# The last dense pass of a graph kernel: centring and scaling on ScalarE, column by column, one pair later

## Chip, cores and metric

One core of one Trainium2 chip runs the whole kernel in one launch. The metric is the device time of that launch in microseconds, the median of several runs. PE is the matrix engine (TensorE), DVE is VectorE, ACT is ScalarE, POOL is GpSimd, SP is SyncE, which here only issues DMAs.

## What is computed

A table `x` of 100,000 nodes with 48 features goes through four rounds of messages over 25,000 edges, each followed by a layer norm. What matters here is the fourth:

```python
gate = silu(edge_attr @ W1.T + b1) @ W2.T + b2 + adapt_logit
msg = gate * h[dst] * (cw * node_mult[dst])[:, None]
agg = segment_sum(msg, src, N) / clip(tot, 1e-8)[:, None]
x = h + agg
y = (x - mean(x)) / sqrt(var(x) + 1e-5) * gamma + beta     # _L3_gnn_ref
out = layernorm(h + y)                                      # the last step of reference()
```

The third round has a dense part too: a node without edges gets `relu(b)` added and is normed. A node that no edge writes to needs no messages, so for most of the table rounds three and four together are a row-wise function of the table after round two.

## The kernel before

Nodes lie 784 to a partition (128 partitions), edges 196 to a partition. **Dense passes** run over all nodes in 28 blocks of 28 rows a partition (a tile half of 128x28x48 = 128x1344 f32), two blocks to a pair: SyncE loads both halves of `din`, VectorE and ScalarE work on them, SyncE stores both halves of `do`. **Sparse rounds** run over the edges in 14 chunks of 14 edges a partition (128x14x48 = 128x672). GpSimd gathers each chunk with 14 indirect DMAs, VectorE forms the messages and sums them with a scan, ScalarE spreads masks and copies the sums back. Rows that edges touch are corrected afterwards by an indirect scatter over the dense result.

The change lies in the last dense pass, `dense_pair` on VectorE (L1563 on) and on ScalarE (L753 on). It does round three's norm, round four's norm with gamma and beta for nodes without edges, and the final norm, for 14 pairs. The pairs are put between the chunks of three sparse rounds, in an order written out by hand that both engines' programs must share:

- `REC_PAIRS = 6`: one pair after every second chunk of the **records round** (`records`, L765 and L1594). Chunks are gathered into two ring buffers (L465); GpSimd fills one again when VectorE has read it (L1596) and ScalarE has stored it (L768).
- `SRC_PAIRS = (2, 3, 4, 5)`: one pair after the 3rd to 6th of the seven blocks of the **h2 round** (L1630 on).
- `LAST_PAIRS = 4`: one pair after every second of the first eight chunks of the **terms round** (`terms_of`, L816 and L1643). Its rows are gathered ahead into four ring buffers (L508), each free again when ScalarE has refilled it (L789, L820).

In one pair VectorE adds the bias (L1566), sums the squares that ScalarE makes (L605, L1570), takes two reciprocals for each half (L1573, L1574) of roots from ScalarE (L757, L759), multiplies (L1577), builds the factor from gamma (L1580), applies it (L1584) and adds beta (L1587). Then `norm` takes the mean (L1343), centres (L1346), sums the second squares (L1352), takes reciprocals (L1355) of ScalarE's roots (L611) and writes the product to `do` (L1363). All full-size VectorE operations are 128x1344, twice a pair.

In SyncE's queue `dense` (L382 on) has the loads of pair n+1 ahead of the stores of pair n, and both ahead of the loads of pair n+2. A load waits for `in_free`, a store for `out_ready`.

After the terms round come `carries` (L1319), a last loop over the 14 chunks (L1690 on, `norm_half`) and the scatter to `out` (L520), which waits until all dense stores have landed.

Of the kernel before, what the change touches and what calls it, by code (L numbers as in the profile page):

```python
# [6 lines left out]
P = 128  # L7
D = 48
# [4 lines left out]
CE = 196  # L13
# [15 lines left out]
SORT_C = 256  # L29
REC_PAIRS, SRC_PAIRS, LAST_PAIRS = 6, (2, 3, 4, 5), 4  # L30
SORT_P = EP // SORT_C
# [58 lines left out]
def bass_gnn(nc, A, OUT):  # L90
    ALU, ACT, X = mybir.AluOpType, mybir.ActivationFunctionType, mybir.AxisListType.X
    ctx = ExitStack()
    with ctx:
# [25 lines left out]
        def blk(table, k, w=D):  # L119
# [107 lines left out]
        back = gflat[:, 0:2 * H * RW].rearrange("p (h c w) -> p h c w", h=2, w=RW)  # L227
        put4 = zs[:, :].bitcast(I32)
        PS = ctx.enter_context(nc.psum_tensor("PS", [P, 8 * 512], F32))
        psT0, psT1, psA, psB, psC, psO0, psG, psS = (PS[:, k * 512:(k + 1) * 512] for k in range(8))  # L230
# [28 lines left out]
            "zt_ready", "zt_st", "z_ld0", "z_ld1", "z_free", "h2_fill0", "h2_fill1", "h2_fill2", "h2_fill3",  # L259
            "h2_free") + ROWS}  # L260
        FROM_DMA = ("look", "g_ld", "g_fill", "g_st", "consts", "edges", "ea48", "xa_ld0", "xa_ld1", "ld0", "ld1",
# [311 lines left out]
        def _(act):  # L573
# [177 lines left out]
            by_src = RECB.rearrange("(p c) w -> p c w", p=P)  # L751

            def dense_pair():  # L753
                squares(pair)
                for h in range(2):
                    act.wait_ge(var_ready.sem, var_ready.up())
                    nc.scalar.activation(std[:, h, :], var[:, h, :], ACT.Sqrt, bias=lneps[:, 0:1], scale=1.0 / D  # L757
                                         ).then_inc(own.sem, own.add())
                    nc.scalar.activation(std2[:, h, :], var[:, h, :], ACT.Sqrt, bias=eps2[:, 0:1],  # L759
                                         scale=(1.0 + EPS) / D).then_inc(own.sem, own.add())  # L760
                    act.wait_ge(own.sem, own.now())
                    act.sem_inc(S["std_ready"], 1)
                norm(pair)

# [10 lines left out]

            record_turn = {own: 4, scanned: 2, spread: 4, returned: 2, fill[0]: H, fill[1]: H, rb_st[0]: 1, rb_st[1]: 1}
            act.wait_ge(S["by_src"], 1)
            for i in range(REC_PAIRS):
                for h in range(2):
                    records(2 * i + h, h)  # L780
                dense_pair()
            for i in range(NBLK - REC_PAIRS):
                for h in range(2):
                    records(2 * (i + REC_PAIRS) + h, h)

# [30 lines left out]
            def terms_of(c, h, last=False):  # L816
# [11 lines left out]
                if not last:  # L828
                    load_back(c + 2, h)

            term_turn = {own: 2, scanned: 2, spread: 4, returned: 2, centered: 2, var_ready: 2, ring_read: 2,
                         rb_ld[0]: 1, rb_ld[1]: 1}
            for i in range(LAST_PAIRS):
                for h in range(2):
                    terms_of(2 * i + h, h)
                dense_pair()
            for i in range(NBLK - 1 - LAST_PAIRS):
                for h in range(2):
                    terms_of(2 * (i + LAST_PAIRS) + h, h)
            for h in range(2):  # L840
                terms_of(CE // H - 2 + h, h, True)

# [174 lines left out]
        def _(dve):  # L1017
# [541 lines left out]
            V.tensor_copy(gammaP, rows[:, 1, :]).then_inc(own.sem, own.add())  # L1559
            one(V.tensor_copy(betaP, rows[:, 2, :]))  # L1560
            dve.sem_inc(S["by_src"], 1)

            def dense_pair():  # L1563
                for h in range(2):
                    dve.wait_ge(ld[h].sem, ld[h].up())
                    V.tensor_tensor(DU[h], wide(h, D), down(rbcP), ALU.add).then_inc(S["centered"], 1)  # L1566
                for h in range(2):
                    dve.wait_ge(squared.sem, squared.up())
                    dve.sem_inc(S["in_free"], 1)
                    V.tensor_reduce(var[:, h, :], sq[:, h, :, :], X, ALU.add).then_inc(S["var_ready"], 1)  # L1570
                for h in range(2):
                    dve.wait_ge(std_ready.sem, std_ready.up())
                    V.reciprocal(srsP[:, h, :], std[:, h, :]).then_inc(own.sem, own.add())  # L1573
                    V.reciprocal(sr2[:, h, :], std2[:, h, :]).then_inc(own.sem, own.add())  # L1574
                dve.wait_ge(own.sem, own.now())
                for h in range(2):
                    V.tensor_tensor(DU[h], DU[h], along(srsP[:, h, :]), ALU.mult).then_inc(own.sem, own.add())  # L1577
                    one(V.tensor_tensor(sr2[:, h, :], sr2[:, h, :], std[:, h, :], ALU.mult))
                for h in range(2):
                    V.tensor_tensor(factorP[:, h, :, :], along(sr2[:, h, :]), down(gammaP), ALU.mult  # L1580
                                    ).then_inc(own.sem, own.add())
                dve.wait_ge(own.sem, own.now())
                for h in range(2):
                    V.scalar_tensor_tensor(DU[h], factorP[:, h, :, :], 1.0, DU[h], ALU.add, ALU.mult).then_inc(own.sem, own.add())  # L1584
                dve.wait_ge(own.sem, own.now())
                for h in range(2):
                    V.tensor_tensor(DU[h], DU[h], down(betaP), ALU.add).then_inc(own.sem, own.add())  # L1587
                dve.wait_ge(own.sem, own.now())
                norm(pair, stores=True)
                for h in range(2):  # L1590
                    st[h].n += 16
                dve.sem_inc(S["out_ready"], 2)

# [6 lines left out]

            pair_turn = {ld[0]: 1, ld[1]: 1, st[0]: 1, st[1]: 1, squared: 4, std_ready: 4}
            PAIR = 4 + 4 + 2 + 2 + 2 + NORM2
            record_turn = {fill[0]: H, fill[1]: H, spread: 4, ring_read: 2}
            for i in range(REC_PAIRS):
                for h in range(2):
                    records(h)
                dense_pair()
            for i in range(NBLK - REC_PAIRS):
                for h in range(2):
                    records(h)  # L1610
            dve.wait_ge(returned.sem, returned.up(2 * NBLK))
# [31 lines left out]
            def terms_of(c, h):  # L1643
# [16 lines left out]

            term_turn = {own: 8, fill[0]: H, fill[1]: H, spread: 4, ring_read: 2, squared: 2, std_ready: 2,
                         rb_ld[0]: 1, rb_ld[1]: 1}
            for i in range(LAST_PAIRS):
                for h in range(2):
                    terms_of(2 * i + h, h)
                dense_pair()
            for i in range(NBLK - LAST_PAIRS):
                if i == NBLK - LAST_PAIRS - 1:
                    counts(nv[:, :])
                for h in range(2):  # L1670
                    terms_of(2 * (i + LAST_PAIRS) + h, h)
            dve.wait_ge(returned.sem, returned.up(2 * NBLK))
# [100 lines left out]
```

## Time and profile before

| | us |
|---|---|
| median of three runs | 2563.16 |
| lowest and highest | 2560.93, 2564.61 |
| the profiled execution, its own time | 2565.39 |
| its span in the trace | 2563.4 |
| DVE busy in the span | 1932.9 (75%) |
| POOL busy | 1781.0 (69%) |
| ACT busy | 618.8 (24%) |
| PE busy | 556.7 (22%) |

The profile is one execution. "Busy" counts the instructions' own time; an engine's idle time before an instruction is given with what ended it. In the timeline, a row is a start, a duration, an engine, a line, what is written from what, how many such instructions are merged ("x2"), and in brackets the idle time before it and what ended it. The records round lies between about 1435 and 1720 us, the h2 round and the products before it between 1720 and 2026, the terms round between 2026 and 2277, the last loop and the scatter after that.

### The profile page before, as it was taken

The page shows a single profiled execution, that of the slowest core. Times are in us where ns is not written, and L with a number is a line of the kernel's source. Part 1 is how long each engine was busy: PE and PEld are TensorE (multiplying, and loading weights), DVE is VectorE, ACT ScalarE, POOL GpSimd, SP SyncE. Part 2 cuts the span into 40 slices and gives each one's busy share as a digit, 9 for nine tenths or more (in the row PEclk, how much of TensorE's full clock was granted, in tenths as well). Part 3 has the DMA queues.
Part 4 walks back from the last instruction along what each step waited for, and adds up shares of the span by engine and source line. Part 5 has one row for each costly group of instructions (what it writes and reads, how often), then busy time and mean ns, then how long its engine had stood idle before and what let it go on. Part 6 is the DMA issues. An engine that isn't in the chain of part 4 may idle for free.

```text
span 2563.4 us, 12772 instructions
## 1 busy us (share of the span) xinstructions
PE 556.7 (22%) x2848; PEld 471.7 (18%) x2848; DVE 1932.9 (75%) x2740; ACT 618.8 (24%) x1106; POOL 1781.0 (69%) x1768
## 2 busy tenths in 40 slices
PE   3800000006787375532310000006200000000000
PEld 1300000006777254432310000006200000000000
DVE  5889999997888675553484099984699999988881
ACT  4910022213443221111110023231112222321110
POOL 4777777775777767737776676767777774637776
PEclk9955555556666576755555555555555555555555
DMA  4169589823445333298009644452232222210000
GB/s 137 21 230 329 156 322 330 299 69 111 158 147 168 104 72 69 51 54 56 17 13 67 87 131 142 124 160 63 50 84 79 82 79 83 65 37 17 17 16 15
DMA packets 158466, 276.19 MB, mean 108 GB/s; under 512 B 88601, under 2 KB 113507, under 8 KB 158259
## 3 DMA queue, kind: packets, MB, share of 16 engines
q1 hardware_dynamic: 96675, 206.39, 28.6%
q0 software_dynamic: 56448, 44.23, 10.3%
q10 hardware_dynamic: 5264, 24.74, 2.7%
q8 instruction: 23, 0.38, 0.1%
q14 instruction: 56, 0.46, 0.1%
HBM read 142.41 MB, written 138.17 MB: 109 GB/s over the span
## 4 chain that ended last, share of the span: by engine, by line
DVE 47%; POOL 20%; issue 9%; PE 8%; DMA 8%; ACT 7%; SPq 1%; ACTq 0%; DVEq 0%; POOLq 0%
POOL out L520 7%; POOL ring L465 7%; POOL x_table L520 6%; DVE PS L1343 5%; PE PS L897 5%; DVE du L1346 5%; DVE var L1352 4%; DVE do L1363 3%; DMA x_table<-sumb,put 3%; PE PS L883 3%; DVE sumb L1271 3%; DMA din<-in_xaux 2%; DMA din<-x_table 2%; ACT GX L661 2%; DVE du L1577 2%
## 5 line engine op out<-in xcount | busy, mean ns | idle before, releaser
L605 ACT ACTIVATE sq<-du 128x1344 f32<-128x1344 f32 x129 | 169.2, 1321 | 541.5 <-DVE du L1346 518.5
L520 POOL DMA_INDIRECT x_table<-sumb,put x196 | 212.5, 1084 | 114.1 <-issue 58.2
L508 POOL DMA_INDIRECT ring<-h_by_src,zs x196 | 204.0, 1041 | 98.8 <-issue 58.5
L478 POOL DMA_INDIRECT XD<-in_xaux,srcI x196 | 201.0, 1025 | 86.3 <-issue 59.1
L520 POOL DMA_INDIRECT out<-sumb,put x196 | 192.6, 982 | 96.5 <-issue 61.8
L465 POOL DMA_INDIRECT ring<-x_with_degree,srcI x196 | 203.7, 1039 | 80.4 <-issue 60.6
L520 POOL DMA_INDIRECT x_with_degree<-sumb,put x196 | 193.8, 989 | 86.7 <-issue 57.3
L465 POOL DMA_INDIRECT ring<-edge_records,dstI x196 | 185.9, 949 | 91.4 <-issue 57.9
L478 POOL DMA_INDIRECT XD<-x_table,srcI x196 | 196.3, 1002 | 59.7 <-issue 59.7
L478 POOL DMA_INDIRECT XD<-xa_table,dstI x196 | 191.1, 975 | 59.7 <-issue 59.4
L866 PE MATMUL PS<-ident,tail 128*49 128x128 f32 x10 | 4.5, 447 | 911.1 <-DVEq L1045 911.1
L1352 DVE TENSOR_REDUCE var<-sq 128x28 f32<-128x1344 f32 x105 | 159.0, 1550 | 36.5 <-ACT sq L605 35.6
L897 PE MATMUL PS<-w1c,hT 98*128 98x96 f32 x784 | 155.5, 365 | 77.4 <-ACT hT L624 74.7
L866 PEld LDWEIGHTS PS<-ident,tail 128*49 128x49 f32 x10 | 1.6, 157 | 913.6 <-DVEq L1045 893.3
L897 PEld LDWEIGHTS PS<-w1c,hT 98*128 98x128 f32 x784 | 147.9, 281 | 82.5 <-ACT hT L624 79.5
L624 ACT ACTIVATE hT<-PS 97x512 f32<-97x512 f32 (+3 forms) x168 | 89.8, 541 | 274.0 <-PE PS L883 273.8
L883 PE MATMUL PS<-ident,din 128*97 128x128 f32 x392 | 94.5, 388 | 256.7 <-DMA din<-x_table 256.7
L883 PEld LDWEIGHTS PS<-ident,din 128*97 128x97 f32 x392 | 75.7, 255 | 259.3 <-DMA din<-x_table 259.3
L1343 DVE TENSOR_REDUCE PS<-du 128x28 f32<-128x1344 f32 x73 | 111.1, 1556 | 3.0
L1346 DVE SCALAR_TENSOR_TENSOR du<-PS,du 128x1344 f32<-128x1344 f32 x73 | 111.0, 1553 | 1.4
L597 ACT ACTIVATE MG<-sumb 128x672 f32<-128x672 f32 x42 | 56.7, 1351 | 192.7 <-DVE sumb L1271 192.7
L983 PE MATMUL PS<-logit,du 120*128 120x120 f32 x392 | 69.9, 352 | 81.0 <-DVEq L1471 81.0
(271 smaller groups left out, 2489.7 us busy)
## 6 DMA issues: line engine op xcount, KB each, us to landing
din<-in_xaux SPq DMA_DIRECT2D x56, 728.0 KB, 5.0
xa_table<-din SPq DMA_DIRECT2D x28, 728.0 KB
x_table<-GX SPq DMA_DIRECT2D x28, 686.0 KB
x_with_degree<-GX SPq DMA_DIRECT2D x28, 686.0 KB
din<-x_table SPq DMA_DIRECT2D x28, 686.0 KB
x_table<-do SPq DMA_DIRECT2D x28, 672.0 KB
din<-x_table SPq DMA_DIRECT2D x28, 672.0 KB
out<-do SPq DMA_DIRECT2D x28, 672.0 KB
```

What stands on the lines that cost most here:

```text
L465: pool.indirect_dma_start(ring[:, h, t, 0:w], None, table, bass.IndirectOffsetOnAxis(ap=of[:, c * H + t:c * H + t + 1], axis=0), **skip).t ...
L478: pool.indirect_dma_start(XD[:, t, 0:w], None, table, bass.IndirectOffsetOnAxis(ap=of[:, t:t + 1], axis=0)).then_inc(rows[c].sem, rows[c]. ...
L508: pool.indirect_dma_start(ring4[:, c % 4, t, :], None, H2, bass.IndirectOffsetOnAxis(ap=of[:, c * H + t:c * H + t + 1], axis=0), bounds_ch ...
L520: pool.indirect_dma_start(table, bass.IndirectOffsetOnAxis(ap=put[:, c * H + t:c * H + t + 1], axis=0), rows_of[:, h, t, :], None, bounds_ ...
L605: nc.scalar.activation(sq[:, h, :, :], u, ACT.Square).then_inc(S["squared"], 1)
L624: nc.scalar.activation(hT[0:tall, g % 2, 0:w], psT[g % 2][0:tall, 0:w], ACT.Copy).then_inc(S["hT_ready"], 1)
L883: last = T.transpose(psT[g % 2][0:tall, j * P:(j + 1) * P], rows_of[:, at:at + tall], ident[:, :])
L897: last = T.matmul(psO[k % 5][:, j * 96:(j + 1) * 96], hT[0:tall + 1, g % 2, j * P:(j + 1) * P], weights[:, :], start=True, stop=True)
L1271: return V.tensor_tensor_scan(sums_row[:, part], by[:, :, :].rearrange("p d c -> p (d c)"), terms_row[:, part], 0.0, ALU.mult, ALU.add)
L1343: V.tensor_reduce(mean[:, h, :], x, X, ALU.add).then_inc(own.sem, own.add())
L1346: V.scalar_tensor_tensor(u, along(mean[:, h, :]), -1.0 / D, x, ALU.mult, ALU.add).then_inc(S["centered"], 1)
L1352: V.tensor_reduce(var[:, h, :], sq[:, h, :, :], X, ALU.add).then_inc(S["var_ready"], 1)
```

## The change

In the dense pairs, the second norm's centring and its product leave VectorE. VectorE still takes the mean (now of the row sums `mu`), and the sum of squares, now of the uncentred values; from both it works out the variance, asks ScalarE for one root of 128x56, and leaves a scale `srs` and a shift `mu` for each row. ScalarE applies both in a new function, `final`, by one activation for each of the 28 columns of each half, with the shift as bias and the scale as scale, and writes `do`. It does so for pair n-1 during pair n, between the roots and the second squares, from two buffers `zbuf` in `gflat`. VectorE's second mean in pair n waits for it (`final`), because it overwrites `mu`. The last pair's `final` stands on ScalarE after chunk 12 of the terms round.

Beta is centred once, ahead of the records round. The stores' `out_ready` comes from ScalarE, half by half. The pairs of the records round stay after chunks 1, 3, 5, 7, 9, 11; those of the terms round go from after chunks 1, 3, 5, 7 to after 1, 4, 7, 10. The h2 round's stay.

```diff
-REC_PAIRS, SRC_PAIRS, LAST_PAIRS = 6, (2, 3, 4, 5), 4
+REC_PAIRS, SRC_PAIRS, LAST_PAIRS = (1, 3, 5, 7, 9, 11), (2, 3, 4, 5), (1, 4, 7, 10)
...
+            def final(n):
+                act.wait_ge(S["scales"], n + 1)
+                for h in range(2):
+                    act.wait_ge(st[h].sem, st[h].now())
+                    for c in range(R):
+                        nc.scalar.activation(do[:, h, c, :], zbuf[n % 2][:, h, c, :], ACT.Identity,
+                                             bias=mu[:, h, c:c + 1], scale=srs[:, h, c:c + 1]
+                                             ).then_inc(own.sem, own.add())
+                    act.wait_ge(own.sem, own.now())
+                    act.sem_inc(S["out_ready"], 1)
+                    st[h].n += 16
+                act.sem_inc(S["final"], 1)
+
             def dense_pair():
-                squares(pair)
+                n = pairs[0]
+                pairs[0] += 1
+                units = [(h, zbuf[n % 2][:, h, :, :]) for h in range(2)]
+                squares(units)
...
-                norm(pair)
+                if n:
+                    final(n - 1)
+                squares(units)
+                act.wait_ge(var_ready.sem, var_ready.up())
+                nc.scalar.activation(std[:, :, :], var[:, :, :], ACT.Sqrt, bias=lneps[:, 0:1], scale=1.0
+                                     ).then_inc(S["std_ready"], 1)
...
+            for c in range(CE // H):
+                terms_of(c, c % 2, c + 2 >= CE // H)
+                if c in LAST_PAIRS:
+                    dense_pair()
+                if c == CE // H - 2:
+                    final(pairs[0] - 1)
...
-            one(V.tensor_copy(betaP, rows[:, 2, :]))
+            one(V.tensor_reduce(mu[:, 0, 0:1], rows[:, 2, :], X, ALU.add))
+            one(V.scalar_tensor_tensor(betaP, mu[:, 0, 0:1].broadcast_to([P, D]), -1.0 / D, rows[:, 2, :],
+                                       ALU.mult, ALU.add))
...
                 for h in range(2):
-                    V.tensor_tensor(DU[h], DU[h], down(betaP), ALU.add).then_inc(own.sem, own.add())
+                    one(V.tensor_tensor(Z[h], Z[h], down(betaP), ALU.add))
+                    dve.sem_inc(S["centered"], 1)
+                if n:
+                    dve.wait_ge(S["final"], n)
+                for h in range(2):
+                    V.tensor_reduce(mu[:, h, :], Z[h], X, ALU.add).then_inc(own.sem, own.add())
+                for h in range(2):
+                    dve.wait_ge(squared.sem, squared.up())
+                    V.tensor_reduce(var[:, h, :], sq[:, h, :, :], X, ALU.add).then_inc(own.sem, own.add())
                 dve.wait_ge(own.sem, own.now())
-                norm(pair, stores=True)
-                for h in range(2):
-                    st[h].n += 16
-                dve.sem_inc(S["out_ready"], 2)
+                one(V.scalar_tensor_tensor(sr2[:, :, :], mu[:, :, :], -1.0 / (D * D), mu[:, :, :], ALU.mult, ALU.mult))
+                V.scalar_tensor_tensor(var[:, :, :], var[:, :, :], 1.0 / D, sr2[:, :, :], ALU.mult, ALU.add
+                                       ).then_inc(S["var_ready"], 1)
+                dve.wait_ge(std_ready.sem, std_ready.up())
+                one(V.reciprocal(srs[:, :, :], std[:, :, :]))
+                V.scalar_tensor_tensor(mu[:, :, :], mu[:, :, :], -1.0 / D, srs[:, :, :], ALU.mult, ALU.mult
+                                       ).then_inc(S["scales"], 1)
```

## Rows read from the trace of the kernel before

**Rows 1.** The page's part 4, the chain that ended last, by engine.
```profile
DVE 47%; POOL 20%; issue 9%; PE 8%; DMA 8%; ACT 7%; SPq 1%; ACTq 0%; DVEq 0%; POOLq 0%
```
**Rows 2.** Busy time by stretch: us, then PE, PEld, DVE, ACT, POOL; clock, DMA.
```profile
1549.01:1711.37 162.36, 0.00 (x0) 0.00 (x0) 150.43 (x128) 48.80 (x80) 109.67 (x116) 0.50 0.45 138
...
2026.50:2276.50 250.00, 0.00 (x0) 0.00 (x0) 230.22 (x226) 78.79 (x119) 154.87 (x150) 0.50 0.25 76
...
2300.60:2563.40 262.80, 0.00 (x0) 0.00 (x0) 172.96 (x220) 36.57 (x65) 192.54 (x196) 0.50 0.06 16
```
**Rows 3.** Timeline of VectorE: one pair of the records round and the readings around it.
```profile
1511.32 1.28 DVE L1596 TENSOR_TENSOR sub<-ring 128x672 f32<-128x672 f32 x1
...
1516.24 2.99 DVE L1566 TENSOR_TENSOR du<-din,PS 128x1344 f32<-128x1344 f32 x2
...
1522.98 0.34 DVE L1573 RECIPROCAL PS<-std 128x28 f32<-128x28 f32 x1 [0.22 <-ACTq L762]
...
1536.08 3.02 DVE L1343 TENSOR_REDUCE PS<-du 128x28 f32<-128x1344 f32 x2
...
1549.01 1.29 DVE L1596 TENSOR_TENSOR sub<-ring 128x672 f32<-128x672 f32 x1
```
**Rows 4.** Timeline of ScalarE in the same pair: last roots, then second squares.
```profile
1522.38 0.32 ACT L757 ACTIVATE std<-var,lneps 128x28 f32<-128x28 f32 x1 [0.93 <-DVE var L1570]
1522.60 0.30 ACT L759 ACTIVATE std<-var,eps 128x28 f32<-128x28 f32 x1
1540.72 2.79 ACT L605 ACTIVATE sq<-du 128x1344 f32<-128x1344 f32 x2 [17.82 <-DVE du L1346]
```
**Rows 5.** GpSimd, records round: who waited for VectorE's reading; last gathers of two chunks.
```profile
  POOL ring L465: 27.1, 5
...
1452.10 0.94 POOL L465 DMA_INDIRECT ring<-edge_records,dstI  x1 [0.30 <-issue]
...
1504.53 0.94 POOL L465 DMA_INDIRECT ring<-edge_records,dstI  x1 [0.30 <-issue]
```
**Rows 6.** The h2 gathers by line: ns min/median/max, first and last start; waits.
```profile
L508 POOL DMA_INDIRECT ring<-h_by_src,zs x196: 992/997/2184, 1963.3 to 2264.9; - x196
...
  ACTq L820: 40.3, 4
```
**Rows 7.** Timeline of VectorE: a reciprocal of 196 columns.
```profile
1724.50 1.39 DVE L1616 RECIPROCAL PS<-t 128x196 f32<-128x196 f32 x1 [0.56 <-ACT t L638]
```
**Rows 8.** ScalarE by form (count, busy us, mean ns), then two pieces of its timeline.
```profile
L661 ACT ACTIVATE GX<-GX 128x128 bf16<-128x128 f32 x196 | 61.9, 386 | 19.4 <-DVEq L1236 17.6 <-PE PS L939 1.7
...
L624 ACT ACTIVATE hT<-PS 96x512 f32<-96x512 f32 x42 | 24.6, 592 | 109.2 <-PE PS L883 109.2
...
L611 ACT ACTIVATE std<-var,lneps,c2s 128x28 f32<-128x28 f32 x28 | 11.5, 409 | 18.9 <-DVE var L1352 18.9
...
L624 ACT ACTIVATE hT<-PS 96x256 f32<-96x256 f32 x14 | 5.3, 381 | 19.8 <-PE PS L883 19.8
...
L638 ACT ACT_TABLE_LOAD x3 | 3.8, 1283 | 0.1
...
99.91 1.26 ACT L661 ACTIVATE GX<-GX 128x128 bf16<-128x128 f32 x4
...
243.35 0.26 ACT L649 ACTIVATE din<-GX 128x28 f32<-128x28 f32 x1 [6.24 <-DMA din<-in_xaux]
243.48 0.24 ACT L650 ACTIVATE din<-GX 128x28 f32<-128x28 f32 x1
```
**Rows 9.** Timeline of VectorE: the first chunk's reading; the step after an h2-round pair.
```profile
1454.61 1.32 DVE L1596 TENSOR_TENSOR sub<-ring 128x672 f32<-128x672 f32 x1 [17.17 <-DMA ring<-edge_records,dstI]
...
2016.34 1.56 DVE L1635 TENSOR_TENSOR du<-XD,MG 128x1344 f32<-128x1344 f32 x1 [0.22 <-DVE do L1363]
```
**Rows 10.** Timeline of ScalarE at the end of the terms round.
```profile
2268.19 1.36 ACT L597 ACTIVATE MG<-sumb 128x672 f32<-128x672 f32 x1 [3.75 <-DVE sumb L1271]
2270.81 0.76 ACT L822 ACTIVATE sq<-du 128x672 f32<-128x672 f32 x1 [1.26 <-DVE du L1650]
```
**Rows 11.** SyncE's own waits: for what, us in total, times, longest.
```profile
SPq L396 <- DMA out<-do: 3.9, 1, 3.9
```

## What I predict, and how it is worked out

> **What bounds the kernel now.** I read the chain of work first. VectorE holds 47% of it [rows 1], and this change lies wholly in the stretch that VectorE holds. By the table of stretches [rows 2], VectorE is busy 150.4 of 162.4 us in the rounds over the edge records after the second pair and 230.2 of 250.0 in the round over the terms. The output scatter from 2300.6 us on is GpSimd's (192.5 of 262.8) and merely starts when VectorE lets it. So a microsecond on VectorE between 1475 and 2300 us moves the end by a microsecond, as long as GpSimd's gathers keep ahead.
>
> Then the timeline of one dense pair. It runs from 1516.24 to 1549.01, 32.77 us, with VectorE never idle but for 0.22 us [rows 3]. ScalarE, in the same pair, has done its roots at 1522.90 (1522.60 + 0.30) and does nothing for 17.82 us until the second squares [rows 4]. That idle stretch is the cover the change wants to use. The question is whether it is long enough.
>
> Gathers: GpSimd waited for VectorE's reading of the ring 5 times, 27.1 us in all, in the records round [rows 5], and four times, 40.3 us in all, for a freed h2 buffer [rows 6]. It is not the bound in any of these rounds now.
>
> **The change on VectorE.** Up to the second mean a pair does what it did: that mean starts 19.84 us after the pair's start [rows 3]. Beta's addition now waits for itself twice instead of once, some 0.04 us for each more wait and 0.1 in all: 19.97 us. From the mean to the next instruction outside the pair it took, in the same timeline, 1549.01 - 1536.08 = 12.93 us: mean 3.05, centring 3.05, second sum of squares 2.93, reciprocals 0.84, product 3.16. Centring and product go. Mean and sum of squares stay (3.05 + 2.93). In place of the rest come two small operations of 128x56, the root, one reciprocal, one more small operation. For each small one I take 0.22 us, between nothing and the 0.34 of a reciprocal of 128x28, with 0.04 between them. The root, ScalarE's 0.32 for 28 columns, is 0.34 with 0.05 and 0.08 for the two handings over. The reciprocal is 0.33 for 28 columns and 1.39 for 196 [rows 3, 7], so 0.51 for 56. With the gaps that is 1.75 us (1.4 to 2.2), and the stretch is 7.73 us. **Without any new wait a pair saves 12.93 - 7.73 - 0.13 = 5.07 us**, 71 us in fourteen.
>
> **The change on ScalarE.** `final` issues 56 activations of 128x48, one for each column, each with its scale and its bias read from a column of a tile. The trace has no such form. Its nearest rows [rows 8]:
> - four of 128x128 with a column as bias: 1.26 us for four, 0.386 for one, so one each 0.291 us. 80 elements fewer at 0.83 ns (512 against 256 columns: 0.592 - 0.381 us) give 0.225.
> - the root of 128x28 with a column as bias: the next one starts 0.22 to 0.23 us later [rows 4]; 20 elements more give 0.242.
> - the second column operand: the root takes 0.409 us with a scale column [rows 8] and 0.32 without [rows 4], 0.09 more. That the first one slows the pace, and not only the single instruction, is seen where neither is a column: 0.13 us from start to start for 128x28, against 0.22 to 0.23.
>
> So the pace is 0.315 to 0.332 us. I take 0.325, the middle rounded up. If the second operand were read beside the first, it would be 0.225 to 0.242; if nothing overlapped, 0.42. A `final` is then 2 x (28 x 0.325 + 0.10) + 0.15 = **18.55 us** (0.10 for the last one's end, 0.15 for the wait between the halves).
>
> The Trainium skill, page "ScalarE: Activation LUTs", section "What ACT_TABLE_LOAD costs", gives 186 ns plus 0.833 ns an element, 93 ns for each column operand, and an overlap of 93 ns; by an estimate from that one starts each 319 ns and the whole sum below would end 4.7 us lower, at 2575.6. By that rule, the trace agrees on all parts but the case of two column operands in a row, which it doesn't show. Its section "Rules for kernel authors" speaks against the change: adds and multiplies belong on VectorE.
>
> **What that does in a pair.** ScalarE starts `final` 6.81 us into the pair (roots done at 6.66), ends it at 25.36, and VectorE, which needs mu back before its mean, goes on at 25.46 instead of 19.97. **It waits 5.49 us.** Queued behind that wait are the mean and all that follows; ScalarE's squares stand behind `final` too, but take 1.36 us each while the mean takes 3.05, so they add nothing. Net for one pair: -5.07 + 5.49 = +0.42 us. In the h2 and terms rounds the product was followed by a wait of 0.22 us [rows 9], which the new last operation lacks: +0.22 there. Sum for pairs 2 to 14: 5 x 0.42 + 8 x 0.22 = +3.9 us.
>
> The first pair has no `final`: -5.07. It would end at 1508.42 - 5.07 = 1503.35 (1508.42 is 2.90 before the fourth chunk's reading at 1511.32 [rows 3]), but the fourth chunk's last gather is issued from 1504.53 to 1505.47. The first chunk's went out from 1452.10 to 1453.04 and was read at 1454.61 [rows 5, 9], 1.6 us later. So the fourth's reading moves from 1511.32 to 1507.1 only: **-4.2 us**.
>
> **The last `final`.** It is no longer inside a pair. ScalarE runs it after the copy back of chunk 12, before its part of chunk 13. That copy ended at 2269.55 [rows 10]. From 2269.65 on it takes 18.55 us, and the square that VectorE waits for in chunk 13 starts at 2288.2 instead of 2270.81: **+17.4 us**, with nothing on VectorE beside it, and carries, the last loop and the scatter all behind it. ScalarE could have done it since the end of the last pair; it is its place in the queue that costs.
>
> **Moved and free.** Spreading pairs over the terms round (after chunks 1, 4, 7, 10 instead of 1, 3, 5, 7): VectorE never waited for a gather there, and with pairs of 33 us GpSimd, at 18.7 us a chunk (from 1963.3 to 2265.9 for 14, less 40.3 of waits [rows 6]), has chunk 13 in at about 2243, some 25 us before it is read. Its waits there are off the path, so this edit is worth nothing here; it would count if pairs became 5 us shorter. Centring beta is two operations of 128x48 before 1454.61, where VectorE sits idle 17.17 us [rows 9]. The stores of a pair go out during the next one, and in SyncE's queue the loads of the pair after that stand behind the second store: issued 26 us into the pair instead of 3. A store was in 3.9 us after its wait began [rows 11]; three such transfers in a row end about 12 us later, at 38, and the next pair begins at 33 + 7.9 = 41. Hidden with 3 us to spare at worst, 10 in the other rounds.
>
> **Sum.** -4.2 + 3.9 + 17.4 = +17.1 us. The profiled execution took 2565.4 us (span 2563.4), so 2582.5; the median of the runs is 2563.2, so **2580.3 us**, 0.7% slower. One hundredth of a microsecond in the pace is 0.56 us fourteen times, 7.8 us. A pace of 0.30 gives 2561, one of 0.35 gives 2600; 4 us more to each side for the small operations make 2556 and 2604.
>
> **Rivals.**
> - *The second column operand costs nothing in pace* (0.242). `final` takes 13.9 us, VectorE waits 0.8, and a pair saves 4.2 to 4.4. Six pairs in the records round: -25.2, near what GpSimd's 27.1 us of waiting allow. Four in the h2 round: -17.6. The terms round then starts at 1984, ends on its own work at 2214, and the last `final` adds 12.9: 2227 instead of 2276.5, so 2514 us. For it: only that no row has two in a row. Against it: the first operand does slow the pace. It decides from a pace of about 0.30 downwards. 0.12.
> - *A pace near 0.30*: some more overlap; VectorE waits 4 us in a pair, the tail costs 16: 2561, within 0.2%. 0.10.
> - *The function of `final` needs another table than the roots*: two loads of 1.28 us [rows 8] a pair, in the wait's path: +2.6 x 14 = 36, 2616 us. Against it: copies and squares ran between roots with no load. 0.04. The Trainium skill (same page, section "Table sets: the hidden batching unit") has identity in every set, which speaks against it too.
> - *No overlap at all between activations with two columns* (0.42): +75, 2655 us. 0.04.
>
> The forecast holds 0.70. The range 2556 to 2604 takes in it and the second rival, and leaves out 0.20. About 0.2%, 5 us, is what a measurement of this kernel tells from no change: faster 0.12, same 0.11 (the second rival and a little of the forecast's low end), slower 0.77.
>
> **What the new profile would show.** Right: 784 new activations of 128x48 at about 0.41 us each, one starting each 0.32; VectorE idle 5 to 6 us before the second mean of thirteen pairs, put down to ScalarE; pairs of 33 us but the first of 28; one idle of 17 us in the last chunk of the terms; scatter beginning near 2318. Wrong: if that idle is under 1 us, the pace was; if table loads stand in the pairs, the third rival is. If VectorE waits for the loads at the head of a pair, SyncE's order was the thing that I costed at nothing.

## The result, and the profile after

The changed kernel takes 2576.4 us (median of 13 runs) where the kernel before took 2564.9 in as many runs beside it: ratio 1.0042, 95% interval 1.003 to 1.0053, so 11 us slower. The forecast was +17.1, with 2580 us.

Part 4 of the page of the changed kernel, the chain that ended last by engine, then its costliest lines:

```profile
DVE 36%; POOL 19%; ACT 17%; DMA 10%; PE 9%; issue 8%; SPq 1%; ACTq 0%; DVEq 0%; POOLq 0%
ACT do L764 10%; POOL out L522 7%; POOL ring L467 6%; POOL x_table L522 5%; PE PS L915 5%; DMA x_table<-sumb,put 3%; DVE PS L1361 3%; DMA din<-in_xaux 3%; PE PS L901 3%; DVE du L1364 3%; DVE sumb L1289 3%; DMA din<-x_table 3%; DVE var L1370 2%; ACT GX L663 2%; DVE mu L1618 2%
```

VectorE had 47% of the chain [rows 1] and has 36. One line of ScalarE, the column activations (L764), now holds 10%, nearly all of its 252 us. VectorE works beside them for most of that time, so the share isn't what they cost; it shows that the work was moved off VectorE and stayed on the path.

Timeline of the changed kernel, second pair of the records round, first VectorE, then ScalarE (start, duration, engine, line, what is written from what, idle time before and what ended it):

```profile
1502.28 2.99 DVE L1591 TENSOR_TENSOR GX<-din,PS 128x1344 f32<-128x1344 f32 x2
...
1519.07 3.25 DVE L1613 TENSOR_TENSOR GX<-GX,PS 128x1344 f32<-128x1344 f32 x2
1527.42 3.01 DVE L1618 TENSOR_REDUCE mu<-GX 128x28 f32<-128x1344 f32 x2 [5.09 <-ACTq L770]
1530.35 3.00 DVE L1621 TENSOR_REDUCE var<-sq 128x28 f32<-128x1344 f32 x2
1533.38 0.22 DVE L1623 SCALAR_TENSOR_TENSOR sr<-mu 128x56 f32<-128x56 f32 x1
1533.63 0.22 DVE L1624 SCALAR_TENSOR_TENSOR var<-var,sr 128x56 f32<-128x56 f32 x1
1534.26 0.50 DVE L1627 RECIPROCAL srs<-std 128x56 f32<-128x56 f32 x1 [0.41 <-ACT std L789]
1534.79 0.22 DVE L1628 SCALAR_TENSOR_TENSOR mu<-mu,srs 128x56 f32<-128x56 f32 x1
1534.93 1.30 DVE L1633 TENSOR_TENSOR sub<-ring 128x672 f32<-128x672 f32 x1
```
```profile
1508.65 0.30 ACT L781 ACTIVATE std<-var,eps 128x28 f32<-128x28 f32 x1
1509.13 18.14 ACT L764 ACTIVATE do<-GX,mu,srs 128x48 f32<-128x48 f32 x56 [0.18 <-ACT std L781]
1527.46 2.54 ACT L607 ACTIVATE sq<-GX 128x1344 f32<-128x1344 f32 x2 [0.19 <-ACT do L764]
```

This pair answers to [rows 3] and [rows 4]. It lasts 1534.93 - 1502.28 = 32.65 us, against 32.77 before. The 17.82 us in which ScalarE idled are filled with 18.14 us of activations, but they begin 6.85 us into the pair, and VectorE needs them at 20. So it waits 5.09 us, in each of thirteen pairs (66.2 us in all), and that is what two full-size operations had saved.

The end of the terms round in the changed kernel, VectorE and then ScalarE, which answers to [rows 10]:

```profile
2257.53 0.86 DVE L1681 SCALAR_TENSOR_TENSOR du<-PS,du 128x672 f32<-128x672 f32 x1
2276.46 0.85 DVE L1684 TENSOR_REDUCE var<-sq 128x14 f32<-128x672 f32 x1 [18.07 <-ACT sq L845]
```
```profile
2255.88 1.36 ACT L599 ACTIVATE MG<-sumb 128x672 f32<-128x672 f32 x1 [3.75 <-DVE sumb L1289]
2257.28 18.13 ACT L764 ACTIVATE do<-GX,mu,srs 128x48 f32<-128x48 f32 x56
2275.66 0.76 ACT L845 ACTIVATE sq<-du 128x672 f32<-128x672 f32 x1 [0.26 <-ACT do L764]
```

The last pair's activations stand alone on the path for 18.13 us. The GpSimd rows by line in the changed kernel (ns min/median/max, then first and last start, then its waits), for the gathers of the records and the last scatter:

```profile
L467 POOL DMA_INDIRECT ring<-edge_records,dstI x196: 940/944/1602, 1426.8 to 1694.2; - x196
...
L522 POOL DMA_INDIRECT out<-sumb,put x196: 969/972/1542, 2305.5 to 2558.8; - x196
```

From the first gather of the records to the first scatter to `out`, the part that the change touches, it takes 2305.5 - 1426.8 = 878.7 us. In the two traces of the kernel before this is 864.9 (2300.6 - 1435.7) and 868.9: 11.8 us more than their mean. The part ahead of 1427 us is the same program in all kernels here and moved by up to 24 us from trace to trace (in the ten traces from chips on which the kernel before takes some 2560 us, the records' gathers begin between 1412.1 and 1435.7), so I compare this stretch and not the spans.

### The profile page after: what moved, and what is told of

Its sections match the earlier page's. It is cut to its first block, busy times and chain, and to the rows that moved or that the text cites. A ratio compares the mean times of both kernels' runs of the same rounds, so it can differ in the third digit from the quotient of the medians.

```text
span 2568.3 us, 13572 instructions
## 1 busy us (share of the span) xinstructions
PE 559.3 (22%) x2848; PEld 472.4 (18%) x2848; DVE 1856.5 (72%) x2713; ACT 865.1 (34%) x1876; POOL 1775.3 (69%) x1768
## 4 chain that ended last, share of the span: by engine, by line
DVE 36%; POOL 19%; ACT 17%; DMA 10%; PE 9%; issue 8%; SPq 1%; ACTq 0%; DVEq 0%; POOLq 0%
ACT do L764 10%; POOL out L522 7%; POOL ring L467 6%; POOL x_table L522 5%; PE PS L915 5%; DMA x_table<-sumb,put 3%; DVE PS L1361 3%; DMA din<-in_xaux 3%; PE PS L901 3%; DVE du L1364 3%; DVE sumb L1289 3%; DMA din<-x_table 3%; DVE var L1370 2%; ACT GX L663 2%; DVE mu L1618 2%
## 5 line engine op out<-in xcount | busy, mean ns | idle before, releaser
L764 ACT ACTIVATE do<-GX,mu,srs 128x48 f32<-128x48 f32 x784 | 252.2, 412 | 4.0 <-ACT std L781 2.3
L607 ACT ACTIVATE sq<-du 128x1344 f32<-128x1344 f32 x73 | 95.4, 1320 | 250.5 <-DVE du L1364 247.5
L915 PE MATMUL PS<-w1c,hT 98*128 98x96 f32 x784 | 148.1, 352 | 74.0 <-ACT hT L626 72.9
L915 PEld LDWEIGHTS PS<-w1c,hT 98*128 98x128 f32 x784 | 141.6, 270 | 78.1 <-ACT hT L626 76.7
L1370 DVE TENSOR_REDUCE var<-sq 128x28 f32<-128x1344 f32 x77 | 116.8, 1550 | 40.3 <-ACT sq L607 39.4
L1618 DVE TENSOR_REDUCE mu<-GX 128x28 f32<-128x1344 f32 x28 | 42.2, 1548 | 66.3 <-ACTq L770 66.2
```

The costliest lines, as they stand in the source:

```text
L607: nc.scalar.activation(sq[:, h, :, :], u, ACT.Square).then_inc(S["squared"], 1)
L764: nc.scalar.activation(do[:, h, c, :], zbuf[n % 2][:, h, c, :], ACT.Identity, bias=mu[:, h, c:c + 1], scale=srs[:, h, c:c + 1]).then_inc(o ...
L915: last = T.matmul(psO[k % 5][:, j * 96:(j + 1) * 96], hT[0:tall + 1, g % 2, j * P:(j + 1) * P], weights[:, :], start=True, stop=True)
L1618: V.tensor_reduce(mu[:, h, :], Z[h], X, ALU.add).then_inc(own.sem, own.add())
```

## Experiments

The theory: two things cost what the change saves. ScalarE starts a column activation each 0.32 us because it reads two column operands, so `final` doesn't fit between the roots and the second mean; and the last `final` stands in ScalarE's queue where nothing covers it. The rivals: the pace has another cause; only the shared `mu` makes VectorE wait; the last `final` is covered or only its store counts; the spreading of the pairs carries part of the result. "Stretch" below is the one from the records' first gather to the first scatter to `out`. Medians differ by some us between chips, so ratios to the kernel before, run beside each, are what counts.

**One column operand.** Half 0 keeps only the bias, half 1 only the scale.

```diff
-                                             bias=mu[:, h, c:c + 1], scale=srs[:, h, c:c + 1]
+                                             bias=mu[:, h, c:c + 1] if h == 0 else 0.0,
+                                             scale=1.0 if h == 0 else srs[:, h, c:c + 1]
```

> The column activations keep only one column operand each: the first half only its bias (scale 1), the second half only its scale (bias 0), so the result isn't the reference's. Theory (each column operand slows the pace of such activations by about 0.09 us, and VectorE's 5.09 us of waiting in a pair is that pace): one starts each 0.23 us instead of 0.32, 56 of them take about 13 us instead of 18.1, the wait before the second mean falls to 0.0 to 0.4 us in thirteen pairs, and the idle in the last chunk of the terms from 18.1 to 13; the median falls by 50 to 62 us, to 2514 to 2526 (GpSimd's gathers may hold some of it back). Rival (only the single instruction gets longer by an operand, the pace is set by something else): pace and waits stay, 2572 to 2580.

Measured 2503.5 us against 2560.0, ratio 0.976 (0.970 to 0.983). ScalarE of this kernel, one pair, then the same two forms in its list (count, busy us, mean ns):

```profile
1498.40 6.42 ACT L764 ACTIVATE do<-GX,mu 128x48 f32<-128x48 f32 x28 [0.18 <-ACT std L782]
1504.94 6.42 ACT L764 ACTIVATE do<-GX,srs 128x48 f32<-128x48 f32 x28
```
```profile
L764 ACT ACTIVATE do<-GX,mu 128x48 f32<-128x48 f32 x392 | 89.8, 319 | 2.4 <-ACT std L782 2.3
L764 ACT ACTIVATE do<-GX,srs 128x48 f32<-128x48 f32 x392 | 89.8, 320 | 1.7
```

28 take 6.42 us, so one starts each (6.42 - 0.32) / 27 = 0.226 us, whether the column is a bias or a scale; with both it is (18.14 - 0.41 - 0.2) / 55 = 0.319, where 0.2 is what the step from one half to the other adds (1504.94 - 1498.40, less 28 x 0.226). One column operand costs 0.093 us of pace. The wait before the mean is gone, a pair lasts 27.7 us, and the stretch is 814.3 us, 64.4 less than in the changed kernel. The rival that left the pace as it is falls. The idle in the last chunk of the terms falls to 12.4 us (13 expected). The gain on the kernel before is 56.5 us, where the expected 2514 to 2526 against 2564.9 had meant 39 to 51. The interval of the ratio, 43 to 78 us, is too wide to tell these apart; the stretch, 64.4 us less where 50 to 62 were expected, says that the gathers held back a little less than I had allowed for.

**The last `final` left out.** Its activations go, its stores stay.

```diff
-                    for c in range(R):
+                    for c in range(R if n < 13 else 0):
```

> The last pair's 56 activations are left out (the last two blocks are stored without them, so the output isn't the reference's); all else stays. Theory (they stand alone on the path, 18.1 us): idle before the last chunk's sum of squares 0.9 us instead of 18.07, median 17 us lower, 2556 to 2562. Rival (the scatter waits for something else, such as the last store, so only part comes back): 2563 to 2576.

Measured 2552.2 us, ratio 0.996 (0.993 to 0.999). The stretch is 858.9 us, 19.8 less, and the idle before the last chunk's sum of squares is back at 0.89 us:

```profile
2256.53 0.85 DVE L1684 TENSOR_REDUCE var<-sq 128x14 f32<-128x672 f32 x1 [0.89 <-ACT sq L845]
```

So the 18 us are its own time; no store stood behind it. The stretch gives 2.6 us more than the 17.2 us of idle that went (18.07 - 0.89). VectorE's waits for the products of the h2 round are 2.7 us shorter in this trace (51.3 us against 54.0 in the changed kernel), and they vary from trace to trace in unchanged code, as the second trace of the kernel before shows further down.

**The last `final` in pieces.** Same work, laid into ScalarE's idle moments of chunks 11 to 13 and behind the last copy.

```diff
+                apply(3 if c >= 11 else 0)
                 act.wait_ge(centered.sem, centered.up())
...
                                      scale=1.0 / D).then_inc(S["std_ready"], 1)
+                apply(10)
                 give_back(c, h)
...
-                if c == CE // H - 2:
-                    final(pairs[0] - 1)
+                if c == 10:
+                    queue.append(steps(pairs[0] - 1))
+            apply()
...
-            dve.wait_ge(S["final"], pairs[0])
...
+            dve.wait_ge(S["final"], pairs[0])
```

`apply(k)` issues the next k activations of the queue. VectorE's wait for them moves from ahead of `carries` to just ahead of the last loop.

> Only the last pair's 56 activations are moved: 10 behind the root and 3 ahead of the square in chunks 11, 12 and 13, the rest after the last copy back, where ScalarE idles over 10 us. VectorE waits for them only ahead of the last loop. Theory (it was the place in the queue that cost 18 us, not the work): 2557 to 2563, idle before each sum of squares of chunks 11 to 13 stays at about 0.9 us. Rival (the pieces push back the roots, the masks or the last loop): each piece that does adds 1 to 3 us a chunk, 2564 to 2574.

Measured 2553.3 us, ratio 0.9965 (0.994 to 0.999). Its ScalarE, chunk 13 and after:

```profile
2257.98 3.27 ACT L765 ACTIVATE do<-GX,mu,srs 128x48 f32<-128x48 f32 x10
2261.83 1.34 ACT L600 ACTIVATE MG<-sumb 128x672 f32<-128x672 f32 x1 [0.58 <-DVE sumb L1306]
2263.21 5.51 ACT L765 ACTIVATE do<-GX,mu,srs 128x48 f32<-128x48 f32 x17
```

Ten activations take 3.27 us and end 0.58 us before the copy back can start. VectorE waits 1.04 us once, ahead of the last loop. The stretch is 861.5 us, 17.2 less than in the changed kernel: the same 56 activations cost 18 us in one place of the queue and 1 in another.

**Pairs packed.** The changed kernel with the terms round's pairs where they were.

```diff
-REC_PAIRS, SRC_PAIRS, LAST_PAIRS = (1, 3, 5, 7, 9, 11), (2, 3, 4, 5), (1, 4, 7, 10)
+REC_PAIRS, SRC_PAIRS, LAST_PAIRS = (1, 3, 5, 7, 9, 11), (2, 3, 4, 5), (1, 3, 5, 7)
```

> The changed kernel with the pairs of the terms round put back to after chunks 1, 3, 5, 7. Theory (with pairs of 33 us VectorE is the bound, spreading is worth nothing): VectorE waits for no gather, median within 3 us of 2576. Rival (spreading carries part of the result, because the last six chunks run without a pair and outrun the gathers): VectorE waits for gathers in chunks 10 to 13, 5 to 15 us more, 2581 to 2591.

Measured 2568.6 us against 2560.0, ratio 1.0028 (0.9999 to 1.0056), whose interval overlaps the changed kernel's. GpSimd's waits for an h2 buffer, 7.6 us in the changed kernel, are 37.6 again, and the stretch is 878.9 us against 878.7. The spreading moved 30 us of GpSimd's waiting and no time.

**Two sets of `mu` and `srs`.** VectorE's mean no longer waits; ScalarE's order stays. `MU` and `SRS` hold two sets each, used in turn, and VectorE waits only at the start of a pair for the `final` of two pairs back.

```diff
+                if n > 1:
+                    dve.wait_ge(S["final"], n - 1)
...
-                if n:
-                    dve.wait_ge(S["final"], n)
                 for h in range(2):
-                    V.tensor_reduce(mu[:, h, :], Z[h], X, ALU.add).then_inc(own.sem, own.add())
+                    V.tensor_reduce(MU[n % 2][:, h, :], Z[h], X, ALU.add).then_inc(own.sem, own.add())
```

> The changed kernel with two sets of mu and srs, so that VectorE's second mean need not wait for the activations of the pair before; ScalarE's order is unchanged. Theory (the squares stand behind the activations in ScalarE's queue, so the wait moves from the mean to the second sum of squares): the mean starts at once, then VectorE idles some 3.4 us before the sum of squares, and a pair is 1.5 us shorter (the mean's 3.0 hidden, 1.4 of a square laid open): 13 x 1.5 = 20 us less than the changed kernel, so some 9 us under the kernel before. Rival (the shared tile is the whole cause): the 5.1 us go, 13 x 5.1 = 66 us less, some 50 under the kernel before.

Measured 2552.4 us against 2557.5, ratio 0.998 (0.997 to 0.999); stretch 864.9 us, 13.8 less. VectorE in one pair of this kernel:

```profile
1521.49 3.01 DVE L1620 TENSOR_REDUCE GX<-GX 128x28 f32<-128x1344 f32 x2
1527.83 3.01 DVE L1623 TENSOR_REDUCE var<-sq 128x28 f32<-128x1344 f32 x2 [3.33 <-ACT sq L609]
```

The wait moved from the mean to the sum of squares and shrank from 5.09 to 3.33 us, as expected: the squares stand behind `final` in ScalarE's queue. The shared tile was the first cause in line, the queue the second, close behind it. Only 14 of the 20 us came through. VectorE's waits for gathered records grew by 12.0 us, from 31.6 to 43.6, and its waits in the same chunks for the masks that ScalarE spreads shrank by 7.3, from 13.0 to 5.7: 5 us of the missing 6 are there.

**The gaps filled.** Two sets, and the activations in pieces everywhere.

```diff
-                if n:
-                    final(n - 1)
+                apply(36)
                 squares(units)
+                apply()
                 act.wait_ge(var_ready.sem, var_ready.up())
...
+                queue.append(steps(n))
...
                 before(c, h)
+                apply(5)
                 give_back(c, h)
```

> Two sets of mu and srs, and the activations of a pair laid into ScalarE's idle time wherever it has some: 5 in each chunk of the records, 10 ahead of each block of the h2 round, 10 in each chunk of the terms, 36 ahead of a pair's second squares, the rest behind them; the last pair's in chunks 11 to 13 and after. Theory (the work fits, only its place in the queue made it wait): no idle before mean or sum of squares in a pair, pairs of 27.7 us, no 18 us at the end; 13 x 5.1 + 18 = 84 us less than the changed kernel, of which the gathers of the records hold back some 13: 70 us, so about 60 under the kernel before, ratio 0.973 to 0.978. Rival (GpSimd becomes the bound in the h2 gathers too): VectorE waits for the last chunks of the terms, ratio 0.980 or above.

Measured 2511.3 us against 2557.5, ratio 0.981 (0.980 to 0.983): 46 us faster than the kernel before, where I had expected 60. The ratio lies where I had put the rival, but not for the rival's reason: VectorE waits for the h2 gathers once, 0.32 us. The stretch is 822.1 us, 56.6 less than the changed kernel's. In a pair VectorE waits for nothing:

```profile
1518.26 3.01 DVE L1636 TENSOR_REDUCE GX<-GX 128x28 f32<-128x1344 f32 x2
1521.19 3.00 DVE L1639 TENSOR_REDUCE var<-sq 128x28 f32<-128x1344 f32 x2
...
1534.14 1.30 DVE L1651 TENSOR_TENSOR sub<-ring 128x672 f32<-128x672 f32 x1 [5.38 <-DMA ring<-edge_records,dstI]
```

But the second reading behind a pair of the records round waits 5.38 us for its gather. Pairs there begin at 1498.0, 1537.6, 1578.3, 1618.8 and 1658.6, so a round lasts 39.6 to 40.7 us, where a pair and two chunks without a wait for gathers make 35.6. From the first pair to the seventh, which takes in all of these rounds, it is 376.7 us (1838.9 - 1462.2), and 377.4 in the changed kernel: the records round gave almost nothing, and the 56 us came from the h2 round, the terms round and the end. GpSimd paces it. It goes on with the next gathers at 1534.92, 1575.14, 1615.48 and 1655.54, each 40 us after the last, and each time it has idled 3.7 to 5.9 us before. The store of the ring, 3.3 us to land in the median, needed up to 10.1, and issued at 1524.73 it would end about when GpSimd goes on:

```profile
DMA to landing us min/median/max: 3.1/3.3/10.1
```
```profile
1534.92 1.23 POOL L469 DMA_INDIRECT ring<-edge_records,dstI  x1 [5.89 <-issue]
```

That the idle ends with the store's landing is my reading; this row names nothing, and in the changed kernel the profile puts four such idle times (20.9 us) to the ring's store.

In this kernel SyncE issues the next loads 25.2 us into a pair (1523.16) and ScalarE the ring's store at 1524.73, right behind them. In the kernel with one column operand the pair is as long, but the second store's activations end sooner, and the loads go out 20.3 us into the pair (1511.81), 6.4 us ahead of the ring's store (1518.21). There the store landed in 5.2 us at most, GpSimd never idled over 2.2 us before a gather of the records, and four rounds lasted 36.0, 37.3, 37.4 and 36.0 us; from the first pair to the seventh it is 357.9 us. The ring's store goes out at the same place in both, 26.7 us into the pair, so its own lateness in ScalarE's queue isn't the difference. In the changed kernel the loads (1527.72) are 6.2 us ahead of the store (1533.89), and it landed in 4.4 us at most. That points to loads, ring store and gathers meeting as the cause of the missing 14 us. It isn't shown: it is a comparison of kernels that differ in more than that.

**The same, pairs packed.** As the previous kernel, with `LAST_PAIRS` (1, 3, 5, 7).

> The same kernel as the one with the gaps filled, but the pairs of the terms round after chunks 1, 3, 5, 7. Theory (spreading pays only when pairs are short, because the last six chunks then run faster than the gathers): VectorE waits for gathers in the last chunks, 4 to 12 us in all, and the time is that much above the spread one. Rival (spreading is worth nothing at this length either): within 2 us of it.

Measured 2509.2 us, ratio 0.981 (0.980 to 0.983); stretch 822.5 us against 822.1. The theory fell: VectorE waited for no gather in the last chunks. With packed pairs GpSimd may start chunk 12 when chunk 8 is read, and from there to the reading of chunk 13 VectorE takes 2201.9 - 2159.5 = 42.4 us, longer than GpSimd's 2 x 18.7 = 37.4 for chunks 12 and 13.

**The kernel before, once more.**

> The kernel before, once more, for a second trace. The first pair began at 1475.7 us in its first trace and between 1455.6 and 1466.7 in five traces of changed kernels, though nothing ahead of it was changed. If the part ahead of the first pair varies from execution to execution, it begins somewhere between 1455 and 1470 here; if it is a property of the kernel, at 1475 again. From there to the first operation behind the terms round: 802 us either way.

The first pair began at 1472.6 us, in neither of the two places, and the distance to the first operation behind the terms round was 806.4 us, not 802. Of the 4 us, 3.6 are VectorE's waiting for the products of the h2 round (54.0 us here, 50.4 in the first trace). The traces of the changed forms have 51.3 to 54.0. So up to 4 us of a comparison of single traces are no effect of a change, and the 11.8 us above, taken against the mean of the two, hold 1.8 us of it.

**Loads first, and the ring's store early.** To test the meeting of the transfers, SyncE's loads of a pair were put ahead of the stores that become ready later, once in the kernel with the gaps filled, once in the changed kernel, and once with the ring's store issued behind the second squares as well. The edit in the first two, in `dense`:

```diff
+                if ahead:
+                    for h in range(2):
+                        load(h, 2 + h, table, w)
                 for i in range(DBLK // 2 - 1):
                     for h in range(2):
-                        load(h, 2 * i + 2 + h, table, w)
+                        if not ahead or i < DBLK // 2 - 2:
+                            load(h, 2 * i + 2 + h + 2 * ahead, table, w)
```

In both, the last dense pass calls it with `ahead` = 1. The third has besides:

```diff
                 squares(units)
+                if early is not None:
+                    keep(early)
                 apply()
```

where `keep(c)` waits for the gathers of chunk c and issues its store.

> The kernel with the gaps filled, and in the last dense pass SyncE issues the loads of a pair ahead of the stores that become ready later (they go out 3 us into a pair instead of 25). Theory (in the records round the loads, the ring's store and the gathers meet at the end of a pair: the store took up to 10.1 us to land and a pair with its two chunks lasted 39.6 us where VectorE's work is 35.6): the store lands in 3.3 us, GpSimd's waits fall from 5 us to 1 or 2 each, the round of pair and two chunks falls to 36 to 37 us, 12 to 17 us less in all, ratio 0.974 to 0.977. Rival (the store of the ring is late by its own place in ScalarE's queue, the loads don't matter): within 3 us of the kernel with the gaps filled, ratio 0.980 to 0.982.

> The changed kernel, and only the loads ahead of the stores in SyncE's queue. Theory (with pairs of 33 us VectorE is the bound in all three rounds, so what the transfers do at the end of a pair is off the path): GpSimd's 20.9 us of waiting for the ring's store fall, VectorE's time doesn't; median within 3 us of the changed kernel, ratio to the kernel before 1.002 to 1.006. Rival (late loads and stores cost the changed kernel something too): ratio under 1.001.

> As the one with the loads first, and ScalarE issues the ring's store of the next chunk behind a pair's second squares, some 6 us before VectorE reads that chunk, instead of behind the root, 1 us before. Theory (after the loads are out of the way, GpSimd's restart still waits 1 to 2 us for this store): up to 1.5 us less in each of five rounds, 3 to 8 us in all, ratio 0.971 to 0.975. Rival (GpSimd's own 35 us for two chunks and the landing of the last gather are the bound already): within 2 us of it.

> The kernel with the gaps filled, the loads ahead of the stores and the ring's store early, once more, since its first execution was on a chip where all engines waited long for reasons that its trace doesn't name. Theory (loads, the ring's store and the gathers met at the end of each pair and cost some 3 to 4 us in each of five rounds): in the records round the ring's store lands in 3.3 us at most 4, GpSimd waits at most 2 us at a time, a pair with its two chunks lasts 36 to 37 us instead of 39.6, ratio to the kernel before 0.971 to 0.977. Rival (GpSimd's own time is the bound and the transfers didn't matter): rounds of 39 us, ratio 0.980 to 0.983. If the activations again start 1.4 us apart instead of 0.32, the run says nothing on either.

All four ran on one chip, on which the kernel before took 3196 and 3209 us instead of some 2560. The ratios were 1.008, 1.025, 1.006 and, for the last again, 1.006. They answer another question. In these traces the matrix engine, VectorE and ScalarE idle between instructions without anything that the profile can name: in the last one VectorE 744 us and ScalarE 1171 us in all, against 8 and 0.5 in the kernel with the gaps filled on another chip. GpSimd's gathers keep their 0.30 us from one to the next. ScalarE in the last one:

```profile
1934.35 0.43 ACT L770 ACTIVATE do<-GX,mu,srs 128x48 f32<-128x48 f32 x1 [0.96 <-issue]
1935.75 0.43 ACT L770 ACTIVATE do<-GX,mu,srs 128x48 f32<-128x48 f32 x1 [0.97 <-issue]
1937.15 0.43 ACT L770 ACTIVATE do<-GX,mu,srs 128x48 f32<-128x48 f32 x1 [0.97 <-issue]
```

Several in a row start each 1.40 us instead of 0.32, and in the same trace others run at the old pace. So these runs say nothing on the meeting of the transfers, and whether loads first would bring the missing us stays open. What they do show is that none of the four wins there: the three with filled gaps are 0.6 to 0.8% slower than the kernel before, and the changed kernel with the loads first, whose activations stand in one block, 2.5%. The many small instructions may be the reason; no run tests it.

## Why the prediction was right

Taken in the order of its steps:

- *VectorE's saving in a pair*, forecast 5.07 us. The first pair, which waits for nothing, lasts 27.74 us (1494.46 - 1466.72) against 32.76, so 5.02: right, but two misses cancel in it. The stretch from the mean to the end of a pair is 7.51 us (1534.93 - 1527.42) instead of 7.73, as I had sized the small operations and the root too high. And the mean starts 20.19 us into the first pair (1486.91 - 1466.72) instead of 19.97: beta's two additions, each waited for, cost more than the 0.13 us that I had added.
- *The pace*, forecast 0.325 within 0.315 to 0.332. It is 0.319, and `final` takes 18.14 us instead of 18.55. The step that mattered most, that the second column operand slows the pace as the first does, is shown by the run with one. An estimate from the figures of the Trainium skill, page "ScalarE: Activation LUTs", section "What ACT_TABLE_LOAD costs", gives 412 ns for 128x48 with two column operands and a start each 319 ns; the trace agrees on both (412 and 319 ns) here. Where I rounded up from my rows, its number was the better one. For the short roots of 128x28 the agreement that I had claimed is looser: the same estimate gives 302 and 395 ns with one and two columns, the rows have 0.32 us and 409 ns [rows 4, 8].
- *The wait*, forecast 5.49, is 5.09. A pair with `final` therefore changes by -0.12 us in the records round, where I had +0.42, and by -0.20 in the terms round (32.90 against 33.10), where I had +0.22 (0.42 - 0.22 is 0.20; the slip is 0.2 us in all). The four of the h2 round last 130.6 us together instead of 131.6, so -1.0. Thirteen pairs give 5 x (-0.12) - 1.0 + 4 x (-0.20) = -2.4 us instead of +3.9. That is nearly the whole of the miss, and 0.40 us of wait, thirteen times, is 5.2 of it: the size of the pace was off by 2%, the mechanism held.
- *The first pair*, forecast -4.2: the fourth chunk is read 31.5 us behind the pair's start (1498.19 - 1466.72) instead of 35.7. Right, and for the reason given; the gather holds it:

```profile
1498.19 1.30 DVE L1633 TENSOR_TENSOR sub<-ring 128x672 f32<-128x672 f32 x1 [0.75 <-DMA ring<-edge_records,dstI]
```

- *The last `final`*, forecast +17.4: 18.07 us of idle where there was 0.91, so +17.2. Right, and it is shown by leaving it out (19.8 us less) and by spreading it (17.2 less).
- *The sum* with the measured terms: -4.2 - 2.4 + 17.2 = +10.6 us. The ratio 1.0042 gives 0.0042 x 2565 = 10.8; the stretch gives 11.8, of which 1.8 are the waits for products.
- *Costed at nothing*: the spreading, shown to be nothing. That it "would count if pairs became 5 us shorter" was wrong: with pairs of 27.7 us it is nothing too. The late loads and stores are nothing here, as VectorE sets the pace, though GpSimd's waits in the records round now end with the ring's store (20.9 us) where they ended with VectorE's reading [rows 5]. I costed them as hidden "with 3 us to spare"; once the waits in the pairs were gone the records round gained nothing, and if the reading above is right it is because they were hidden no longer.
- *The rivals*: that the second operand is free is refuted by the pace, and so are one near 0.30 and one of 0.42. No table load stands in a pair; the trace has six in all, as before, the last at 1121 us. The first rival's time of 2514 was a good reading of what a pace of 0.24 would give: the run with 0.226 took 2503.5.

## What to carry to other kernels

Ask of moved work not only whether it fits into the idle time of the other engine but whether it is done when its result is needed: 18 us fitted an idle stretch of 18, and were due 5 us earlier. Work that is pipelined one step back needs its own buffers for every tile that it reads, small ones too, and should go into the in-order queue in pieces at the moments when that engine waits; in one block at the end it has no cover at all. Both together turned a change that lost 0.4% into one that gains 1.9%.

## What the runs showed of the hardware

- A column operand, bias or scale, costs 0.093 us of a ScalarE activation's pace: 128x48 with one starts each 0.226 us (0.319 alone), with two each 0.319 (0.412 alone).
- A 693 KB store that lands in 3.3 us in the median took up to 10.1 in the kernel where it is issued 1.6 us behind two 672 KB loads, and up to 5.2 and 4.4 in those where they are 6.4 and 6.2 us ahead. That the loads are the cause is not shown.
- The same program took 25% longer on one chip (3196 and 3209 us against some 2560 on the others). The forms of the change traced there idle about 1 us between many of ScalarE's instructions, and on VectorE and the matrix engine too, without a row that explains it, and all lost to the kernel before. The kernel before has no trace there.
